# Four-layer kernel: ternary gate and up weights rounded into spent SBUF, and the first codes, turns and gate product of layer 1's feed-forward moved into the attention before it

## The chip, the cores and the metric

The kernel runs on one core of one Trainium2 chip. The time is device microseconds of one launch; the kernel's number is the median of three runs. TensorE is called PE in rows, VectorE DVE, ScalarE ACT, GpSimd POOL, and SyncE, which issues the DMAs, SP.

## What is computed

The input x has 2 x 256 rows of 512, in the kernel four tiles of 128 rows (0 and 1 are the first batch). Four layers follow, each an attention-like part and a feed-forward part on a layer norm of x, both added to x. The change touches layer 1: the end of its attention (a latent attention with 16 heads over 512 context rows) and its feed-forward part, which uses 4-bit and 8-bit activations and ternary weights. Cut to what matters:

```python
def int4_quant(x):
    beta = mean(abs(x), axis=-1)
    x_q = clip(round(x * SQRT7 / (beta + EPS)), -8, 7)
    return x_q * (beta * SQRT7) / SQRT7
def int8_quant(x):
    gamma = max(abs(x), axis=-1)
    x_q = clip(round(x * 127.0 / (gamma + EPS)), -128, 127)
    return x_q * gamma / 127.0
def bitlinear(x, w, scale):
    w_mean = mean(abs(w))
    w_q = clip(round(w / (w_mean + EPS)), -1.0, 1.0)
    return einsum('...i,oi->...o', x, w_q * w_mean * scale)
# layer 1, feed-forward, on h = layernorm(x):
#   gate, up = bitlinear(int4_quant(h), w_gate), bitlinear(int4_quant(h), w_up)   512 -> 1376
#   inner    = relu(gate)**2 * up
#   x        = x + bitlinear(int8_quant(inner), w_down)                           1376 -> 512
```

## The kernel before

Each part of a layer is one block: every engine has its own instruction stream, written out by hand in program order, synchronised by semaphores, and all engines meet at a barrier between two blocks. There is no planner; an engine executes its instructions in the order in which they are written.

**Ternary weights.** `TernaryWeights` holds 13 pieces: four of w_gate, four of w_up (128 x 1376 each) and five of w_down (three of 128 x 1536, then 128 x 512 and 96 x 512). Each is loaded twice into one of two raw buffers `tw_raw`: first for the sum of magnitudes, then, during layer 1's attention, for rounding. The second pass is `ternary_round_gpsimd` (lines 391 to 405): three operations of GpSimd for each piece, the last of which writes bf16 codes into one of two buffers `tw_rounded`, while `ternary_round_sync` (line 408) issues the store of each piece to DRAM (`ternary`) and the next load. In the feed-forward block SyncE loads all codes back (lines 1263 to 1269): `wgu` for gate and up in six DMAs, `wd` for down in two; then the first weights of layer 2's key/value and query products.

**The attention's end.** `layer1_attention` goes through 64 units u (tile u // 16, head u % 16). In unit u TensorE makes the scores of unit u + 3, turns the probabilities of u (line 978) and mixes four heads at a time (`mix`, line 994); VectorE takes the maximum of unit u + 3 (line 1072) and copies every fourth turned unit (line 1096); ScalarE does the exponential of u + 2 (line 1176) and the other copies (line 1185). A tile's result is copied by ScalarE (`copy_mixed`), turned by TensorE (`turn_mixed`, line 1008), divided and added to x by VectorE (lines 1082 and 1089). The norm statistics of tiles 0 to 2 are made in units 26, 42 and 58, their inverse roots by GpSimd behind all rounding, their normed rows `xn` by VectorE in units 59, 60 and 62 (`tile_rows_vector`, line 267).

**The feed-forward block.** `layer1_ffn`, for tiles t and the three column chunks c of 1376 (512, 512, 352):

- ScalarE sums the magnitudes of the normed rows (line 1290); VectorE makes the 4-bit codes of two tiles at a time (`quantise4`, lines 1333 to 1353: three small operations, two each of scale, round and clip of 128 x 512, three small ones for the scales), and behind the second pair come four counts of a bisection that belongs to layer 3 (line 2396); TensorE turns the codes (`turn4`, line 1424) and ScalarE copies them out.
- `gate_up(t)` (line 1453): for each chunk eight matmuls, gate and then up, into two banks each; it may write chunk i when ScalarE and VectorE have read chunk i - 2. ScalarE makes relu and square (lines 1311 and 1316), VectorE multiplies with up (`inner_chunk`, line 1365).
- VectorE: `magnitude(t)` (line 1370, the maximum over 1376, and four small ones), `scaled(t)` (line 1380), `rounded(t)` (line 1385), with the chunks of tile t + 1 in between. TensorE turns the 8-bit codes (`turn8`, line 1437), ScalarE copies them in two halves (lines 1300 to 1303), `down(t)` (line 1466) multiplies, and VectorE adds to x (`update`, line 1389).
- TensorE's order of calls is: gate_up 0, turn4 2, turn4 3, gate_up 1, turn8 0, gate_up 2, down 0, turn8 1, gate_up 3, down 1, turn8 2, a first product of layer 2, down 2, another, turn8 3, another, down 3. GpSimd meanwhile splits the loaded weights of layer 2 (`first_group_split`, lines 1524 to 1533).
- The updates of tiles 2 and 3 stand at the start of the next block (line 2295).

## Time and profile before

| what | us |
|---|---|
| median of 3 runs (lowest, highest) | 849.52 (848.99, 854.66) |
| profiled execution | 852.24 |
| its span | 850.5 |
| busy TensorE, VectorE, ScalarE, GpSimd in the span | 773.9, 688.9, 517.5, 431.8 |

The span runs from the first to the last instruction of the profiled execution; times inside it count from its start. Layer 1's attention ends at about 184 us of it, the feed-forward block at about 231.8.

### The profile page before, as it was taken

What the parts mean: (1) busy time and instruction counts of PE and PEld (TensorE: products, weight loads), DVE (VectorE), ACT (ScalarE), POOL (GpSimd) and SP (SyncE); (2) the same over time, 40 slices, a digit from 0 to 9 for tenths busy, and PEclk for the clock granted to TensorE, in tenths of its full rate; (3) what the DMA queues carried; (4) which work ended last, traced back from release to release, by engine and by line L of the source; (5) the groups of instructions that cost most, each with busy time, mean ns of one, the idle gap of its engine ahead of it and who ended that gap; (6) DMA issues with size and microseconds to landing.
All of it is one profiled execution on the core that took longest, in us unless ns stands there. A gap on an engine that the chain in (4) does not pass through costs nothing. (4 is left out here: it accounts for less than half of the span.)

```text
span 850.5 us, 16376 instructions
## 1 busy us (share of the span) xinstructions
PE 773.9 (91%) x5134; PEld 629.5 (74%) x5140; DVE 688.9 (81%) x1766; ACT 517.5 (61%) x1401; POOL 431.8 (51%) x388
## 2 busy tenths in 40 slices
PE   1986799948988999999999999999999999978888
PEld 0484676634677898888888888989888889866347
DVE  7877898979787887887887888788878878876986
ACT  6865789846457657657657656665675675641421
POOL 3136158824135754755746646745754764665110
PEclk9998899989999999999999999999999999999999
DMA  8245136635020320220220320310310210004001
GB/s 308 100 132 180 53 137 217 195 113 184 12 89 1 101 76 1 99 74 0 99 74 0 99 74 0 99 62 13 99 50 25 74 50 25 26 1 120 2 0 50
DMA packets 37773, 66.15 MB, mean 78 GB/s; under 512 B 5537, under 2 KB 17889, under 8 KB 37602
## 3 DMA queue, kind: packets, MB, share of 16 engines
q1 hardware_dynamic: 37730, 65.63, 23.2%
q8 instruction: 21, 0.34, 0.2%
q14 instruction: 22, 0.18, 0.1%
HBM read 60.28 MB, written 5.34 MB: 77 GB/s over the span
## 5 line engine op out<-in xcount | busy, mean ns | idle before, releaser
L2396 DVE TENSOR_SCALAR_CACHE_REDUCE xn<-ctxT,candidate 128x512 bf16<-128x512 f32 x240 | 168.9, 742 | 0.0
L2043 ACT ACTIVATE layer_attention_probs<-xnT,stats 128x512 f32<-128x512 f32 x128 | 93.9, 733 | 113.5 <-DVE stats L2178 113.5
L2190 DVE TENSOR_TENSOR layer_attention_probsT<-bank,layer_attention_probsT 128x512 fp32r<-128x512 f32 x128 | 88.2, 689 | 50.5 <-ACT layer_attention_probsT L2051 49.3
L1782 PE MATMUL bank<-layer_attention_keysT,layer_attention_queriesT 128*128 128x512 f32 x384 | 121.1, 423 | 4.9 <-DVE layer_attention_queriesT L2171 4.9
L1782 PEld LDWEIGHTS bank<-layer_attention_probsT,layer_attention_values 128*128 128x128 f32 x768 | 99.1, 190 | 13.7 <-DVE layer_attention_probsT L2190 4.2
L2051 ACT CAST layer_attention_probsT<-bank 128x512 fp32r<-128x512 f32 x128 | 74.9, 585 | 52.8 <-PE bank L1859 52.8
L1782 PE MATMUL bank<-layer_attention_probsT,layer_attention_values 128*128 128x256 f32 x768 | 102.6, 283 | 4.4 <-DVE layer_attention_probsT L2190 2.2
L1782 PE MATMUL bank<-layer_attention_l_wq,layer_attention_xnT 128*128 128x512 f32 x408 | 99.3, 392 | 0.1
L1782 PEld LDWEIGHTS bank<-layer_attention_l_wkv,layer_context_parts 128*128 128x128 f32 x720 | 88.4, 188 | 2.7
L1782 PE MATMUL bank<-layer_attention_l_wkv,layer_context_parts 128*128 128x256 f32 x720 | 90.4, 278 | 0.0
L1782 PE MATMUL bank<-layer_attention_wo,layer_attention_headsT 128*128 128x512 f32 x336 | 88.8, 406 | 0.0
L2178 DVE CUSTOM_DVE_ANT_0 xnT<-bank,layer_attention_mask 128x512 f32<-128x512 f32 x128 | 87.2, 681 | 0.6 <-PE bank L1782 0.5
L1782 PEld LDWEIGHTS bank<-layer_attention_l_wq,layer_attention_xnT 128*128 128x128 f32 x408 | 75.3, 188 | 15.9 <-issue 0.2
L1725 POOL TENSOR_TENSOR layer_attention_mixed<-layer_attention_mixed,xnT 128x512 f32<-128x512 f32 x30 | 49.1, 1637 | 69.9 <-DVE candidate L2446 41.7
L1859 PE MATMUL bank<-ident,layer_attention_probs 128*128 128x128 f32 x512 | 76.9, 272 | 3.0 <-ACT layer_attention_probs L2043 3.0
L1859 PEld LDWEIGHTS bank<-ident,layer_attention_probs 128*128 128x128 f32 x512 | 61.3, 140 | 14.4 <-issue 4.0
L1782 PEld LDWEIGHTS bank<-layer_attention_keysT,layer_attention_queriesT 128*128 128x128 f32 x384 | 62.6, 190 | 11.4 <-issue 5.7
L1782 PEld LDWEIGHTS bank<-layer_attention_wo,layer_attention_headsT 128*128 128x128 f32 x336 | 60.0, 189 | 11.5
L1710 POOL TENSOR_SCALAR layer_attention_ssq<-layer_attention_ssq 128x4 f32<-128x4 f32 x48 | 9.7, 203 | 87.5 <-ACT layer_attention_squares L2002 87.5
L2002 ACT ACTIVATE layer_attention_squares<-bank 128x128 f32<-128x128 f32 x192 | 52.0, 298 | 0.0
L1712 POOL TENSOR_TENSOR layer_attention_ssq<-layer_attention_ssq,minus_half 128x4 f32<-128x4 f32 x48 | 48.9, 1018 | 4.0
L1715 POOL TENSOR_TENSOR xn<-xn,layer_attention_ssq 128x512 f32<-128x512 f32 x47 | 48.9, 1040 | 3.7
(340 smaller groups left out, 1639.6 us busy)
## 6 DMA issues: line engine op xcount, KB each, us to landing
layer_attention_l_raw_qo<-in_wqT SPq DMA_DIRECT2D x8, 1024.0 KB, 5.5
layer_attention_l_raw_qo<-in_woT SPq DMA_DIRECT2D x8, 1024.0 KB, 6.0
xnT<-inverse_sums SPq DMA_DIRECT2D x15, 512.0 KB, 3.7
tw_raw<-in_w_gateT SPq DMA_DIRECT2D x8, 688.0 KB, 5.4
tw_raw<-in_w_upT SPq DMA_DIRECT2D x8, 688.0 KB, 4.3
tw_raw<-in_w_downT SPq DMA_DIRECT2D x6, 768.0 KB, 4.7
layer_attention_l_raw_kv<-in_wkvT SPq DMA_DIRECT2D x8, 512.0 KB, 4.7
ternary<-tw_rounded SPq DMA_DIRECT2D x8, 344.0 KB, 2.6
```

Source lines behind the costliest of these rows:

```text
L1710: own(g.tensor_scalar(ssq[:, c, :], ssq[:, c, :], 1.0 / HD, EPS, ALU.mult, ALU.add))
L1712: own(g.tensor_tensor(ssq[:, c, :], ssq[:, c, :], k.minus_half[:, 0:REP], ALU.pow))
L1715: g.tensor_tensor(r, r, ssq[:, c, :].unsqueeze(2).broadcast_to([P, REP, HD]), ALU.mult)\
L1725: g.tensor_tensor(now, now, factors, ALU.mult).then_inc(S_["mix_scaled"], 1)
L1782: last = pe.matmul(out, stationary[f][a], moving[f][b], start=f == 0 and x == 0, stop=f == count - 1 and x == 2)
L1859: last = pe.transpose(T[u % 2][:, c * P:(c + 1) * P], probs[:, u % 3, c * P:(c + 1) * P], k.ident[:, :])
L2002: return a.activation(squares[:, h, :], source, ACT.Square, accum_out=ssq[:, c, h:h + 1])
L2043: a.activation(probs[:, u % 3, :], masked[:, u % 2, :], ACT.Exp, bias=negmax[:, u:u + 1], scale=-1.0, accum_out=sums[:, u:u + 1]).then_inc ...
L2051: a.copy(probsT[:, 0, p % 2, :, u % 2 * P:(u % 2 + 1) * P], T[u % 2][:, :].rearrange("p (c q) -> p c q", c=CPB)).then_inc(S_["probsT_high" ...
L2178: v.tensor_tensor_reduce(masked[:, u % 2, :], S[u % 2][:, :], mask[:, u % TPB, :], -1.0, 3.4e38, ALU.add, ALU.min, negmax[:, u:u + 1]).the ...
L2190: v.tensor_tensor(probsT[:, 1, p % 2, :, columns], T[u % 2][:, :].rearrange("p (c q) -> p c q", c=CPB), probsT[:, 0, p % 2, :, columns], A ...
L2396: own(k.nc.vector.tensor_scalar((k.flags if flags is None else flags)[:, r % 2], row_tile(k.ctxT, r), k.candidate[:, r:r + 1].bitcast(F32) ...
```

## The change

- The gate and up codes no longer go through DRAM. GpSimd writes them straight into their place in SBUF (`GateUp.weights`), which lies over buffers that the attention has done with. Pieces are rounded in a new order (`ROUNDED`): down first, then up and gate. Piece 0 waits until all queries are made, piece 6 until the first batch's values are used. Only the down codes are stored and loaded back. GpSimd makes the inverse roots of tiles 0 and 1 between pieces.
- The 4-bit codes of tiles 0 and 1 are made in the attention block: one magnitude sum on ScalarE in unit 60, the other on VectorE in unit 61, the rest of the codes on VectorE in unit 62 and behind unit 63; their buffers lie over spent queries. TensorE turns them behind the last `mix`, ScalarE copies them behind its last `copy_mixed`, and TensorE does the first chunk of gate and up of tile 0 as the block's last work, with a wait for all 13 rounded pieces.
- In the feed-forward block the normed rows of tile 2 are made at the start, those of tile 3 behind the first `inner` chunk; the codes of tiles 2 and 3 come within VectorE's work on tile 1 (between its chunks 1 and 2), that is, behind tile 0's 8-bit codes. TensorE does down 0 and turns the late codes ahead of gate_up 2. The four counts move to the end of VectorE's stream. GpSimd's split waits until the late codes' scales are ready.

In the following rows a name such as `layer_attention_codes` is a tile, `x8` at a row's end a count of equal instructions. First TensorE, before, from the last mixing products of the attention into the feed-forward block:

```order
L994 MATMUL bank<-layer_attention_probsT,layer_attention_values 32x128 x24
L1008 MATMUL bank<-ident,layer_attention_mixedT 128x128 x4
L925 UNCONDITIONAL_BRANCH
L1417 UNCONDITIONAL_BRANCH
L1424 MATMUL bank<-ident,layer_ffn_x 128x128 x8
L1453 MATMUL bank<-layer_ffn_wgu,layer_ffn_x4T 128x512 x16
L1453 MATMUL bank<-layer_ffn_wgu,layer_ffn_x4T 128x352 x8
```

The same place of TensorE's stream now (`layer_attention_turned` holds the turned codes of tiles 0 and 1, `layer_attention_gate_up` the gate and up weights):

```order
L1119 MATMUL bank<-layer_attention_probsT,layer_attention_values 32x128 x24
L174 MATMUL bank<-ident,layer_attention_codes 128x128 x8
L1133 MATMUL bank<-ident,layer_attention_mixedT 128x128 x4
L190 MATMUL bank<-layer_attention_gate_up,layer_attention_turned 128x512 x8
L1047 UNCONDITIONAL_BRANCH
L1523 UNCONDITIONAL_BRANCH
L190 MATMUL bank<-layer_attention_gate_up,layer_attention_turned 128x512 x8
L190 MATMUL bank<-layer_attention_gate_up,layer_attention_turned 128x352 x8
```

The turns of the codes and the first eight products now stand ahead of the two branches, which are the border of the blocks.

VectorE, before, in tile 1 of the feed-forward block, from the scaling of tile 0 to the maximum of tile 1:

```order
L1380 TENSOR_SCALAR layer_ffn_inner<-layer_ffn_inner,layer_ffn_ginv 128x1376
L1365 SCALAR_TENSOR_TENSOR layer_ffn_inner<-bank,layer_ffn_up_scale,layer_ffn_gate 128x512
L1385 TENSOR_SCALAR layer_ffn_x<-layer_ffn_inner 128x1376
L1365 SCALAR_TENSOR_TENSOR layer_ffn_inner<-bank,layer_ffn_up_scale,layer_ffn_gate 128x512
L1365 SCALAR_TENSOR_TENSOR layer_ffn_inner<-bank,layer_ffn_up_scale,layer_ffn_gate 128x352
L1370 TENSOR_REDUCE layer_ffn_gamma<-layer_ffn_inner 128x1
```

The same place now, from the second chunk of tile 1 on:

```order
L1464 SCALAR_TENSOR_TENSOR layer_ffn_inner<-bank,codes_up_scale,layer_ffn_gate 128x512
L135 TENSOR_SCALAR codes_beta<-codes_beta 128x2
L137 TENSOR_SCALAR codes_betae<-codes_beta 128x2
L139 RECIPROCAL codes_binv<-codes_betae 128x2
L145 TENSOR_SCALAR layer_ffn_t<-xn,codes_binv 128x512 x2
L151 TENSOR_SCALAR layer_ffn_t<-layer_ffn_t 128x512 x2
L157 TENSOR_SCALAR layer_ffn_x<-layer_ffn_t 128x512 x2
L162 TENSOR_SCALAR codes_betae<-codes_beta 128x2
L164 TENSOR_SCALAR codes_up_scale<-codes_betae,tw_wscale 128x2
L165 TENSOR_SCALAR codes_gate_scale<-codes_betae,tw_wscale 128x2
L1464 SCALAR_TENSOR_TENSOR layer_ffn_inner<-bank,codes_up_scale,layer_ffn_gate 128x352
L1469 TENSOR_REDUCE layer_ffn_gamma<-layer_ffn_inner 128x1
```

The codes of tiles 2 and 3 have moved from the block's start to between the second and third chunk of tile 1.

The diff, cut to its core:

```diff
@@ TernaryWeights @@
+    ROUNDED = (8, 9, 10, 11, 12, 4, 5, 0, 1, 2, 3, 6, 7)
+    OVER_QUERIES, OVER_VALUES = 0, 6
...
+        k.gate_up = GateUp(k, -(-k.nc.sbuf_base // 32) * 32)
@@ ternary_round_gpsimd @@
-    for i, (w, f, rows, width) in enumerate(tw.PIECES):
...
-        g.tensor_scalar(tw.rounded[0:rows, n % 2, 0:width], raw, -ROUND, 1.0, ALU.add, ALU.mult)\
-         .then_inc(tw.rounded_ready, 1)
+        if w == DOWN:
+            if j >= 2:
+                g.wait_ge(tw.stored[n % 2], 16 * (j // 2))
+            target = tw.rounded[0:rows, n % 2, 0:width]
+        else:
+            if tw.ROUNDED[j] == tw.OVER_QUERIES:
+                g.wait_ge(queries_made, B * HEADS1 // 2)
+            if tw.ROUNDED[j] == tw.OVER_VALUES:
+                g.wait_ge(quads_done, TPB * HEADS1 // 4)
+            target = k.gate_up.weights[:, w, f, :]
+        g.tensor_scalar(target, raw, -ROUND, 1.0, ALU.add, ALU.mult).then_inc(tw.rounded_ready, 1)
@@ layer1_attention, gpsimd @@
-                ternary_round_gpsimd(k)
-                for t in range(TILES - 1):
-                    tile_norm_gpsimd(k, following, t)
+                ternary_round_gpsimd(k, 0, 6, S_["queries_psum"], S_["quads_done"])
+                tile_norm_gpsimd(k, following, 0)
+                ternary_round_gpsimd(k, 6, 10, S_["queries_psum"], S_["quads_done"])
+                tile_norm_gpsimd(k, following, 1)
+                ternary_round_gpsimd(k, 10, len(TernaryWeights.PIECES), S_["queries_psum"], S_["quads_done"])
+                tile_norm_gpsimd(k, following, 2)
@@ layer1_attention, tensor @@
                 mix(UNITS // 4 - 1, range(CPB))
+                for t in range(TPB):
+                    codes_turn_tensor(k, t, early_codes[t], code_bank(t))
                 turn_mixed(TILES - 1)
+                pe.wait_ge(k.codes.turned_ready, 1)
+                pe.wait_ge(k.ternary.rounded_ready, len(TernaryWeights.PIECES))
+                gate_up_tensor(k, 0, 0)
@@ layer1_attention, vector @@
-                    if u in (59, 60, 62):
-                        tile_rows_vector(k, following, (59, 60, 62).index(u))
+                    if u in (59, 60):
+                        tile_rows_vector(k, following, (59, 60).index(u))
+                    if u == 61:
...
+                        v.tensor_reduce(k.codes.beta[:, 1:2], k.xn[:, 1, :], AX.X, ALU.add, apply_absolute_value=True)\
+                         .then_inc(k.codes.beta_ready, 1)
+                    if u == 62:
+                        codes_inverse_vector(k, 0)
+                        codes_scaled_vector(k, 0, scaled)
...
+                codes_rounded_vector(k, 0, scaled)
+                codes_clipped_vector(k, 0, scaled, early_codes)
+                codes_scales_vector(k, 0)
                 divide_mixed(TILES - 1)
                 add_mixed(TILES - 1)
@@ layer1_attention, scalar @@
+                    if u == 60:
+                        codes_magnitude_scalar(k, following, 0, absolute)
...
                 copy_mixed(TILES - 1)
+                for t in range(TPB):
+                    codes_turned_scalar(k, t, code_bank(t))
@@ layer1_ffn, sync @@
-                for c, (c0, c1) in enumerate(CHUNKS):
-                    for w in (GATE, UP):
-                        sp.dma_start(wgu[:, w, :, c0:c1], tw.scratch[w].rearrange("(f p) c -> p f c", p=P)[:, :, c0:c1])\
-                          .then_inc(loaded[c], 16)
@@ layer1_ffn, gpsimd @@
+                g.wait_ge(q.scales_ready, 2)
                 first_group_split(k)
@@ layer1_ffn, scalar @@
                     if t == 0:
-                        x4T_copy(2)
-                        x4T_copy(3)
+                        for late in range(TPB, TILES):
+                            codes_magnitude_scalar(k, n, late, absolute[:, late - TPB, :])
                     if t >= 1:
                         x8T_copy(t - 1)
+                    if t == 1:
+                        codes_turned_scalar(k, 2, code_bank(2))
+                        codes_turned_scalar(k, 3, code_bank(3))
@@ layer1_ffn, vector @@
-                quantise4(0)
-                tile_rows_vector(k, n, TILES - 1)
-                quantise4(1)
+                tile_rows_vector(k, n, 2)
...
-                bisection_count(k, own, 0, first_flags(k))
-                for c in range(NC):
-                    inner_chunk(0, c)
-                    if c == 0:
-                        bisection_count(k, own, 1, first_flags(k))
+                inner_chunk(0, 0)
+                tile_rows_vector(k, n, TILES - 1)
+                inner_chunk(0, 1)
+                inner_chunk(0, 2)
...
+                    if t == 0:
+                        codes_inverse_vector(k, 1)
+                        codes_scaled_vector(k, 1, scaled_late)
+                        codes_rounded_vector(k, 1, scaled_late)
+                        codes_clipped_vector(k, 1, scaled_late, codes_late)
+                        codes_scales_vector(k, 1)
...
+                bisection_count(k, own, 0, first_flags(k))
                 for t in range(TPB):
                     tile_rows_vector(k, following, t)
+                bisection_count(k, own, 1, first_flags(k))
@@ layer1_ffn, tensor @@
                 gate_up(0)
-                turn4(2)
-                turn4(3)
                 gate_up(1)
                 turn8(0)
+                down(0)
+                codes_turn_tensor(k, 2, codes_late[0], code_bank(2))
+                codes_turn_tensor(k, 3, codes_late[1], code_bank(3))
                 gate_up(2)
-                down(0)
                 turn8(1)
                 gate_up(3)
                 down(1)
```

The functions `codes_...` are the old `quantise4`, `turn4` and `x4T_copy` taken apart; `gate_up_tensor` is the body of the old loop for one chunk.

## Rows read from the trace of the kernel before

**Rows 1.** Busy us by stretch: PE, PEld, DVE, ACT, POOL; PE clock, DMA share, GB/s

```profile
170.00:184.00 14.00, 9.35 (x131) 5.85 (x129) 9.81 (x25) 6.93 (x17) 4.19 (x7) 1.00 0.11 35
184.00:192.30 8.30, 1.91 (x11) 1.23 (x13) 6.57 (x22) 3.63 (x10) 0.57 (x1) 0.50 0.88 272
192.30:231.80 39.50, 36.38 (x222) 20.51 (x224) 32.41 (x61) 21.23 (x38) 13.34 (x10) 0.98 0.29 91
```

**Rows 2.** Waits in 184 to 200 us: total us, times, longest

```profile
PE bank L1424 <- DVE layer_ffn_x L1347: 6.3, 1, 6.3
```

**Rows 3.** Timeline of the attention's end: start, length in us, instruction, idle before

```profile
176.89 0.69 ACT L1176 ACTIVATE layer_attention_probs<-bank,layer_attention_negmax 128x512 f32<-128x512 f32 x1
181.52 0.63 PE L1008 MATMUL bank<-ident,layer_attention_mixedT 128*128 128x128 f32 x4 [0.80 <-ACT layer_attention_mixedT L1192]
```

**Rows 4.** Timeline of the feed-forward block's start, DVE and PE

```profile
184.25 0.69 DVE L257 BATCH_NORM_STATS2 stats<-x 128x6 f32<-128x512 f32 x1 [0.59 <-PEq L925]
190.53 0.17 DVE L1333 TENSOR_SCALAR layer_ffn_beta<-layer_ffn_beta 128x2 f32<-128x2 f32 x1 [0.79 <-ACT layer_ffn_t L1290]
194.13 0.74 DVE L2396 TENSOR_SCALAR_CACHE_REDUCE xnT<-ctxT,candidate 128x512 bf16<-128x512 f32 x1
191.42 4.78 PE L1453 MATMUL bank<-layer_ffn_wgu,layer_ffn_x4T 128*128 128x512 bf16 x15 [1.99 <-ACT layer_ffn_x4T L1285]
198.35 3.61 PE L1453 MATMUL bank<-layer_ffn_wgu,layer_ffn_x4T 128*128 128x512 bf16 x16 [0.19 <-DVE layer_ffn_inner L1365]
```

**Rows 5.** Groups by shape in 184 to 232 us: count, busy us, mean ns, idle before

```profile
L1311 ACT ACTIVATE layer_ffn_relu<-bank,layer_ffn_gate_scale 128x512 f32<-128x512 f32 x8 | 5.5, 690 | 3.3 <-PE bank L1453 3.2
L1290 ACT ACTIVATE layer_ffn_t<-xn 128x512 f32<-128x512 f32 x4 | 2.5, 621 | 6.5 <-DVE xn L267 3.6 <-PEq L925 2.9
L1365 DVE SCALAR_TENSOR_TENSOR layer_ffn_inner<-bank,layer_ffn_up_scale,layer_ffn_gate 128x512 f32<-128x512 f32 x8 | 6.0, 744 | 1.3 <-ACT layer_ffn_gate L1316 1.3
```

**Rows 6.** Timeline: the four `magnitude` starts, VectorE's largest gap, the block's end

```profile
198.96 1.59 DVE L1370 TENSOR_REDUCE layer_ffn_gamma<-layer_ffn_inner 128x1 f32<-128x1376 f32 x1
205.43 1.59 DVE L1370 TENSOR_REDUCE layer_ffn_gamma<-layer_ffn_inner 128x1 f32<-128x1376 f32 x1
212.03 1.59 DVE L1370 TENSOR_REDUCE layer_ffn_gamma<-layer_ffn_inner 128x1 f32<-128x1376 f32 x1
216.44 0.75 DVE L1365 SCALAR_TENSOR_TENSOR layer_ffn_inner<-bank,layer_ffn_up_scale,layer_ffn_gate 128x512 f32<-128x512 f32 x1 [1.34 <-ACT layer_ffn_gate L1316]
221.00 1.59 DVE L1370 TENSOR_REDUCE layer_ffn_gamma<-layer_ffn_inner 128x1 f32<-128x1376 f32 x1
220.90 0.78 PE L1437 MATMUL bank<-ident,layer_ffn_x 128*128 128x128 bf16 x11
228.86 2.55 PE L1466 MATMUL bank<-layer_ffn_wd,layer_ffn_x8T 128*128 128x512 bf16 x10
231.85 0.75 DVE L2295 SCALAR_TENSOR_TENSOR x<-bank,down_scale,x 128x512 f32<-128x512 f32 x1 [3.62 <-PEq L1259]
```

**Rows 7.** Timeline of GpSimd: its first rounding operation and the first behind all

```profile
112.97 1.48 POOL L400 TENSOR_SCALAR tw_raw<-tw_raw,tw_bound 128x1376 f32<-128x1376 f32 x1 [25.23 <-DVEq L388]
175.13 1.58 POOL L274 TENSOR_TENSOR rstd<-varep,minus_half 128x1 f32<-128x1 f32 x3
```

**Rows 8.** Line 1385 on VectorE (ns min/median/max), and GpSimd's split on the timeline

```profile
L1385 DVE TENSOR_SCALAR layer_ffn_x<-layer_ffn_inner x4: 867/992/1281, 202.6 to 224.1; 128x1376 bf16<-128x1376 f32 x4
203.06 3.01 POOL L1527 TENSOR_TENSOR layer_attention_l_wkv<-layer_attention_l_raw_kv,layer_attention_l_wkv 128x512 fp32r<-128x512 f32 x2
```

**Rows 9.** Busy us by stretch, as in rows 1, in the attention's first part

```profile
96.00:98.00 2.00, 0.42 (x3) 0.42 (x4) 1.94 (x4) 0.78 (x2) 0.00 (x0) 1.00 0.34 94
98.00:100.00 2.00, 2.00 (x17) 1.21 (x16) 1.97 (x4) 1.60 (x3) 0.00 (x0) 0.66 0.01 4
```

**Rows 10.** DMA issues: count, KB each, median us from issue to landing

```profile
layer_ffn_wd<-ternary SPq DMA_DIRECT2D x1, 1280.0 KB, 10.3
tw_raw<-in_w_upT SPq DMA_DIRECT2D x7, 688.0 KB, 4.3
```

More of the change, by code:

```diff
@@ new lines, in codes_scales_vector @@
+def codes_scales_vector(k, h):
+    v, own, q, half, wscale = k.nc.vector, k.vown, k.codes, half_of(h), k.ternary.wscale
+    own(v.tensor_scalar(q.betae[:, half], q.beta[:, half], SQRT7, 1.0 / SQRT7, ALU.mult, ALU.mult))
+    own.wait()
+    own(v.tensor_scalar(q.up_scale[:, half], q.betae[:, half], wscale[:, UP:UP + 1], None, ALU.mult))
+    own(v.tensor_scalar(q.gate_scale[:, half], q.betae[:, half], wscale[:, GATE:GATE + 1], None, ALU.mult))
+    own.wait()
+    v.engine_nop().then_inc(q.scales_ready, 1)
@@ new lines, in codes_turn_tensor, with codes_turned_scalar @@
+def codes_turn_tensor(k, t, codes, bank):
+    pe = k.nc.tensor
+    pe.wait_ge(k.codes.codes_ready, t + 1)
+    for f in range(KT):
+        last = pe.transpose(bank.bitcast(BF16)[:, f * P:(f + 1) * P], codes[:, f * P:(f + 1) * P], k.ident16[:, :])
+    last.then_inc(k.codes.turned_psum, 1)
+def codes_turned_scalar(k, t, bank):
+    a = k.nc.scalar
+    a.wait_ge(k.codes.turned_psum, t + 1)
+    a.copy(k.gate_up.turned[t], bank.bitcast(BF16).rearrange("p (f c) -> p f c", f=KT)).then_inc(k.codes.turned_ready, 1)
@@ L105, in at, with gate_up_tensor @@
+def gate_up_tensor(k, t, c):
+    pe, q = k.nc.tensor, k.codes
+    c0, c1 = INNER_CHUNKS[c]
+    i = len(INNER_CHUNKS) * t + c
+    for w, bank, ready in ((GATE, k.bank[0:2], q.gate_psum), (UP, k.bank[2:4], q.up_psum)):
+        for f in range(KT):
+            last = pe.matmul(bank[i % 2][:, 0:c1 - c0], k.gate_up.turned[t][:, f, :], k.gate_up.weights[:, w, f, c0:c1],
+                             start=f == 0, stop=f == KT - 1)
+        last.then_inc(ready, 1)
 def at(step, per, c):
@@ L286, with __init__, place @@
 GATE, UP, DOWN = range(3)
+INNER_CHUNKS = [(c, min(c + 512, INNER)) for c in range(0, INNER, 512)]
+class GateUp:
+    def __init__(self, k, base):
+        self.begin = base + 4 * KT * (2 * GW2 + 2 * 2 * HD2 + 2 * HD2 + GW2)
+        self.held = 2 * 2 * KT * INNER
+    def place(self, k):
+        view = lambda name, shape, offset: k.nc.alloc_sbuf_tensor_at(k.label + name, [P] + shape, BF16,
+                                                                     offset=self.begin + offset)
+        self.weights = view("gate_up", [2, KT, INNER], 0)
+        early = view("turned", [KT, TPB * P], self.held)
+        self.turned = [early[:, :, t * P:(t + 1) * P] for t in range(TPB)]
 class TernaryWeights:
@@ L2884, in build @@
 def build(nc, dram, out):
-    ternary = [nc.dram_tensor(f"ternary{w}", (INNER, D) if w == DOWN else (D, INNER), BF16, kind="Internal").ap()
-               for w in range(3)]
+    ternary = nc.dram_tensor("ternary", (INNER, D), BF16, kind="Internal").ap()
     inverse = nc.dram_tensor("inverse_sums", (P, 8), F32, kind="Internal").ap()
```

201 lines of the change are left out of this document (97 added, 104 removed).

## The prediction

> **What bounds the kernel now.** I read the views in the order in which they narrow down. The table by stage comes first [rows 1]: from 170 to 184 us (the end of layer 1's attention) and from 192.3 to 231.8 us (its feed-forward part, FFN below) TensorE is busy, but between them, 184.0 to 192.3, it works 1.91 of 8.30 us at a granted clock of 0.50, while the DMA engines are busy 0.88 of the time. The list of waits says for what: one wait of 6.3 us for `layer_ffn_x`, the 4-bit codes that VectorE makes [rows 2]. The first long product starts at 191.42, two more microseconds on, and its 15 matmuls take 4.78 us; 16 of the same kind take 3.61 us at full clock [rows 4]. So the boundary is a serial chain: sum of magnitudes on ScalarE, codes on VectorE, transposes, copy, first product, and all of it behind the barrier between two blocks. After it the FFN is bound by VectorE (32.41 of 39.50 us) and TensorE (36.38) by turns [rows 1]. The next stage starts when TensorE's last product of the FFN is done: VectorE waits 3.62 us for that barrier [rows 6]. From there on the program is unchanged, so what the boundary and the FFN give goes through to the end. Nothing else of the 850 us has to be looked at but the gaps on GpSimd before [rows 7].
>
> **The end of the attention: what is added.** ScalarE gets one magnitude sum (0.62 us by the mean of four [rows 5]) between exponential 62 and the copy of turn 60. It paces this stretch: the last exponential, at 176.89, shows no idle time of ScalarE ahead of it [rows 3], so 0.6 us goes onto the path to the last mixing product. VectorE gets a reduction, the three small operations and the six of 128x512 of the codes: the group from its first small operation at 190.53 to the next work at 194.13 takes 3.60 us [rows 4]. The reduction and the first part fit into its idle time before the last copy of turned probabilities, the rest while TensorE mixes and ScalarE copies; I count nothing for it. If it were not hidden at all, it would cost all 3.6. TensorE turns eight 128x128 of codes in the time in which it waited for the copy of the mixed rows, up to its transpose at 181.52 [rows 3]; then, behind that transpose and ScalarE's copies of the turned codes, eight matmuls of 128x512, half of 3.61, 1.8 us. VectorE's division and addition of the last tile run beside them; I put TensorE's end 0.5 us after theirs. Nothing is queued behind this product in the block, but the barrier waits for it. Sum: the barrier moves from 184.25 to about 185.35, +1.1. Bounds: +0.6 (product hidden) to +4.7 (codes not hidden).
>
> **GpSimd and SyncE.** GpSimd rounds the 13 pieces from 112.97 to 175.13, 62.2 us, loads included [rows 7]. The order of pieces changes, the arithmetic does not; eight stores of 344 KB to DRAM and the six loads back go. Two of its three inverse roots move in between the pieces, each wanted only near 175.7. SyncE issues a load behind fewer stores. I leave the end at 175, within 3 either way. The new wait, the first gate product for all 13 pieces, then ends 8 us before TensorE comes to it, at about 183: no cost. The waits for spent queries and spent values stand at pieces 8 and 12 of the row, at about 149 and 168, when the first half of the attention is over; none either. In the FFN SyncE issues the down weights first. Before they landed 10.3 us after the issue, behind the gate and up weights [rows 10]; even with that they are there at 196, and the first down product wants them at 197.
>
> **The start of the FFN.** VectorE at 185.35: statistics of tile 3 (0.69 and two short ones, as the 0.17 at 190.53), rows of tile 2 (taken as 0.55, under the 0.74 of an `inner` chunk), the first `inner` chunk (0.74) [rows 4, 5]. That ends at 187.8 and lets TensorE into the third chunk. Half of its matmuls (352/512 of half of 1.8 us, 0.6), relu and square (each under the 0.69 of a relu of 512 columns [rows 5]), the last chunk of `inner`: `magnitude(0)` starts at 190.25, where it stood at 198.96 [rows 4, 6]. The lead is 8.7 us. It is made of the codes and their turns that are gone from here (to 191.42), the half clock, the four counts behind 194.13, and it pays the 1.1.
>
> **What is given back.** The codes of tiles 2 and 3 now stand between two chunks of tile 1: +3.60 to 205.43 - 198.96 = 6.47 [rows 6], less what that stretch holds beyond its instructions, a wait for ScalarE and GpSimd's interference, which I put at 0.7: 9.3 us. Lead 5.9. Tile 2's product can only start when its codes are turned behind the first down product, at about 200.3; by my schedule `magnitude(2)` then comes at 206.45 against 212.03, lead 5.6. Between `magnitude(2)` and `magnitude(3)` there were 8.97 us, in part because TensorE did the first down product ahead of the second turn; that product now lies earlier, and I get 7.95: lead 6.6. The four counts (2.9 us with the gaps) now stand at VectorE's end, where it waited 3.62 us for TensorE [rows 6]: they are hidden with about 1 us to spare. TensorE's tail, from its turn at 220.90 to the end of the last down product (228.86 and 2.55), takes 10.5 us and is unchanged; it starts at 214.1, after the last gate and up products at 211.7 and 2.4 us of down product, 6.8 earlier. I take a gain of 6.5 at the FFN's end (6.3 by the ready times of the last codes, 6.8 by the tail).
>
> **Interference.** The operation that rounds 128x1376 to codes took 0.87 us at best and 1.28 at worst [rows 8], the slow ones beside GpSimd's split of the next weights (two operations in 3.01 us). Before three such pairs (scale or round) lay beside the split, now four. By these rows that is 0.1 to 0.4 us more, inside my rounding. The Trainium skill ("SBUF — State Buffer", the term "shared port pair") says that VectorE and GpSimd lock that pair for a whole instruction and that the loser fully blocks. By that rule the extra operation could stand behind one whole split operation, 1.5 us, and the time would be 844.5 rather than 843.0. The rows, with 0.41 us as the largest excess, speak for the smaller figure.
>
> **Sum.** +1.1 at the barrier, -9.8 from the barrier to `magnitude(0)`, +2.8 for the late codes, about -0.6 for the order of TensorE: -6.5 us. The profiled execution took 852.24 us (span 850.5); it becomes 845.7. The median shown, 849.52, lies 2.72 lower: 843.0 us. That is 0.77% less. A measurement of this kernel can tell about 1% (8.5 us) from no change.
>
> **Rivals.**
> (a) The clock falls. Between 96 and 98 us TensorE was busy 0.42 of 2 us, and the next two microseconds had a clock of 0.66 [rows 9]; between 184 and 192.3 it was 0.50 [rows 1]. The new boundary still has a barrier, a wait for the first `inner` and waits of about 1 us in tiles 0 and 1. At half clock a product of eight takes 3.4 instead of 1.8 us; two of them on the path are 3.2 us: 846.2. Against it: no new gap is as long as 2 us. The Trainium skill ("TensorE: Matmul & The Clock Gate", What's actually happening) says that throttled is the default and activity lifts it; that speaks for neither here without the trace.
> (b) The lead carries through. If TensorE's new order and the early start of the down product take the 3.6 us of late codes into waits that were there anyway, 8.7 or more remains: 840.8. For it: VectorE idled 3.62 at the end. Against it: the largest gap of VectorE inside the FFN is 1.34 us, at 216.44 [rows 6].
> (c) Slower: the rounding ends late. Place: TensorE's wait for all 13 pieces at about 183, with the next block's barrier behind it. The loads of one piece are hidden behind the rounding of another only by two buffers. If each of the eight gate and up pieces waited for a whole landing of 4.3 us [rows 10], GpSimd would end 34 us late, at 209, and the time be 843 + 26 = 869. It costs nothing up to 183 and turns the gain over from an end at 189.5. Against it: the whole 62.2 us held 13 pieces with only short gaps [rows 7], and DMA traffic gets less. Gaps of 2 us behind the two small pieces are to be expected.
>
> **How the numbers follow.** Forecast 60%, with its own range 841 to 845.5: each of four stretches is good to about 1 us. (a), together with codes not wholly hidden in the attention's end, 20%, up to 848. (b) 16%, from 839 to 841. (c) 4%. The range 839 to 848 leaves out (c), the far end of (a), where both bounds meet (+4.7 at the barrier and a fallen clock), and the far end of (b). Faster by over 1% means below 841.0: (b) and the edge of the forecast, 0.2. Slower by over 1%: (c), 0.04. Within 1%: 0.76.
>
> **What would show it.** The next profile should have the wait of 6.3 us gone, the granted clock near 1.00 from 184 to 200, the first gate product ending at about 184.7 with GpSimd done at 175, `magnitude` starts near 190.3, 199.6, 206.5 and 214.4, the late codes of 3.6 us between two chunks, and the first operation of layer 2 on VectorE at about 225.4 with a short wait. The prediction is wrong if GpSimd's last piece comes after 183, if the barrier comes after 187, or if the stage behind the FFN gets longer by what the FFN saved.

## The result: faster by half a per cent, two waits larger than forecast

The changed kernel takes 848.77 us (median of 13 runs, 844.14 to 851.61) beside 853.23 us for the kernel before in the same session (13 runs, 848.99 to 855.45): ratio 0.9949, 95% interval 0.9928 to 0.9971. Timed again later it was 847.13 beside 852.7, ratio 0.9938 (0.9917 to 0.9959). So the gain is 4.5 to 5.6 us; the forecast was 6.5 us, ratio 0.9923, and an absolute time of 843.0 with a range that ended at 848. Of the absolute miss of 5.8 us, 3.7 are the yardstick: the kernel before has 849.52 in the three runs shown ahead of the prediction, 853.23 in the 13 runs beside the changed kernel, and medians of 851 to 853 in later sessions. The other 2 us are gain that didn't come.

The profiled execution took 848.75 us, span 846.6. VectorE on the timeline, against [rows 4, 6]: start, length, instruction, idle time ahead of it.

```profile
187.43 0.69 DVE L347 BATCH_NORM_STATS2 stats<-x 128x6 f32<-128x512 f32 x1 [0.66 <-PEq L1047]
192.42 1.59 DVE L1469 TENSOR_REDUCE layer_ffn_gamma<-layer_ffn_inner 128x1 f32<-128x1376 f32 x1
201.78 1.59 DVE L1469 TENSOR_REDUCE layer_ffn_gamma<-layer_ffn_inner 128x1 f32<-128x1376 f32 x1
209.19 1.59 DVE L1469 TENSOR_REDUCE layer_ffn_gamma<-layer_ffn_inner 128x1 f32<-128x1376 f32 x1
217.23 1.59 DVE L1469 TENSOR_REDUCE layer_ffn_gamma<-layer_ffn_inner 128x1 f32<-128x1376 f32 x1
227.76 0.75 DVE L2386 SCALAR_TENSOR_TENSOR x<-bank,down_scale,x 128x512 f32<-128x512 f32 x1 [1.16 <-PEq L1397]
```

Executions differ by up to 5 us in where they stand at 170 us, together with dips of the granted clock ahead of it, and by almost 5 us behind the FFN. So I compare distances and not positions, from a mark that both kernels have: VectorE's reading of the fourth count in the attention's last part, which starts at 170.90 in the kernel before and at 170.12 in the changed one. All distances are from start to start, in us:

| | count to barrier | to magnitude(0) | (0) to (1) | (1) to (2) | (2) to (3) | to layer 2 | sum |
|---|---|---|---|---|---|---|---|
| before | 13.35 | 14.71 | 6.47 | 6.60 | 8.97 | 10.85 | 60.95 |
| forecast | 14.45 | 4.9 | 9.3 | 6.9 | 7.95 | 11.0 | 54.5 |
| changed | 17.31 | 4.99 | 9.36 | 7.41 | 8.04 | 10.53 | 57.64 |
| changed, again | 17.69 | 5.00 | 9.35 | 7.41 | 8.03 | 10.53 | 58.01 |

In these steps the changed kernel gains 3.3 and 2.9 us, less than the medians' 4.5 and 5.6; the rest lies outside them, and no run here says where it comes from.

Four of six steps are right within 0.5 us. Two are not: 2.9 us too much ahead of the barrier, 0.5 between magnitude(1) and (2). The first is seen on the timeline of the changed kernel, all engines, rows of the bisection's update, of GpSimd's rounding and of what waits:

```profile
170.12 0.08 DVE L2487 DVE_READ_ACCUMULATOR xn<-ctxT,candidate 128x1 f32 x1
170.43 1.41 POOL L509 TENSOR_SCALAR tw_raw<-tw_raw,tw_winv 128x1376 f32<-128x1376 f32 x1
170.66 1.20 DVE L2534 TENSOR_TENSOR found<-found,set_bit 128x8 int32<-128x8 int32 x1
171.93 1.34 POOL L521 TENSOR_SCALAR layer_attention_gate_up<-tw_raw 128x1376 bf16<-128x1376 f32 x1
171.97 1.31 DVE L2537 TENSOR_TENSOR candidate<-found,bits 128x8 int32<-128x8 int32 x1
173.92 0.69 ACT L1316 ACTIVATE layer_attention_probs<-bank,layer_attention_negmax 128x512 f32<-128x512 f32 x1 [4.36 <-DVE layer_attention_negmax L1202]
174.75 0.80 PE L1095 MATMUL bank<-l_keysT,layer_attention_queriesT 128*128 128x512 f32 x1 [3.60 <-ACT layer_attention_probs L1316]
```

Two operations on eight columns take 1.20 and 1.31 us. Each ends where the GpSimd operation beside it ends (170.43 + 1.41 = 171.84; 171.93 + 1.34 = 173.27). Behind them VectorE's maximum is late, ScalarE idles 4.36 us, TensorE 3.60. In the kernel before the same two lines on the timeline are

```profile
171.41 0.17 DVE L2443 TENSOR_TENSOR found<-found,set_bit 128x8 int32<-128x8 int32 x1
171.69 0.17 DVE L2446 TENSOR_TENSOR candidate<-found,bits 128x8 int32<-128x8 int32 x1
```

and GpSimd was idle there, in a gap of 2.33 us in which it waited for the small last down piece, between 170.58 and 172.91. The change puts the gate and up pieces last and so a wide rounding under the update. The busy table by stretch of the changed kernel (columns as in [rows 1]) shows the granted clock fall behind TensorE's idle piece, from 1.00 in [rows 1] to 0.75, while 184 to 192.4 runs at 1.00 and not at 0.50:

```profile
170.60:184.00 13.40, 9.54 (x114) 6.26 (x113) 12.05 (x26) 6.87 (x18) 3.13 (x3) 0.75 0.00 0
184.00:192.40 8.40, 7.43 (x43) 3.58 (x42) 6.20 (x15) 5.65 (x11) 0.78 (x1) 1.00 0.42 143
192.40:227.80 35.40, 30.73 (x199) 17.73 (x197) 33.14 (x64) 18.27 (x34) 13.24 (x10) 1.00 0.16 52
```

The second excess lies beside GpSimd's split; VectorE and GpSimd on the timeline of the changed kernel, against [rows 8]:

```profile
202.29 2.50 POOL L1618 TENSOR_TENSOR layer_attention_l_wkv<-layer_attention_l_raw_kv,layer_attention_l_wkv 128x512 fp32r<-128x512 f32 x2
203.91 1.62 DVE L1479 TENSOR_SCALAR layer_ffn_inner<-layer_ffn_inner,layer_ffn_ginv 128x1376 f32<-128x1376 f32 x1
204.73 2.55 POOL L1621 CAST layer_attention_l_wq<-layer_attention_l_raw_qo 128x2048 fp32r<-128x2048 f32 x1
206.11 1.90 DVE L1484 TENSOR_SCALAR layer_ffn_x<-layer_ffn_inner 128x1376 bf16<-128x1376 f32 x1
219.36 0.94 DVE L1479 TENSOR_SCALAR layer_ffn_inner<-layer_ffn_inner,layer_ffn_ginv 128x1376 f32<-128x1376 f32 x1
220.33 0.88 DVE L1484 TENSOR_SCALAR layer_ffn_x<-layer_ffn_inner 128x1376 bf16<-128x1376 f32 x1
```

The same two operations take 1.62 and 1.90 us for tile 1, 0.94 and 0.88 for tile 3, where GpSimd is idle. Over tiles 1 and 2 the excess is 2.2 us (1.62 + 1.90 + 1.02 + 1.28 against twice 0.94 + 0.87). The kernel before already has 0.8 of it: 1.11 us for rounded(0), 1.08 for scaled(1), 1.28 for rounded(1). So the change adds 1.4.

### The profile page after: what moved, and what is told of

Same layout as the page of the kernel before. It is cut to its first block and busy times, and to the rows that moved or that the text cites. A ratio compares the mean times of both kernels' runs of the same rounds, so it can differ in the third digit from the quotient of the medians.

```text
span 846.6 us, 16363 instructions
## 1 busy us (share of the span) xinstructions
PE 776.7 (92%) x5140; PEld 633.9 (75%) x5140; DVE 692.8 (82%) x1767; ACT 517.6 (61%) x1399; POOL 431.9 (51%) x388
## 5 line engine op out<-in xcount | busy, mean ns | idle before, releaser
L2142 ACT CAST layer_attention_probsT<-bank 128x512 fp32r<-128x512 f32 x128 | 75.0, 586 | 54.7 <-PE bank L1950 54.5
L1873 PE MATMUL bank<-layer_attention_l_wkv,layer_context_parts 128*128 128x256 f32 x720 | 93.5, 282 | 0.0
L1873 PEld LDWEIGHTS bank<-layer_attention_l_wkv,layer_context_parts 128*128 128x128 f32 x720 | 91.1, 188 | 2.5
L1316 ACT ACTIVATE layer_attention_probs<-bank,layer_attention_negmax 128x512 f32<-128x512 f32 x64 | 44.8, 705 | 11.8 <-DVE layer_attention_negmax L1202 11.5
```

Of the source, the lines that this page charges most:

```text
L1316: a.activation(probs[:, u % 4, :], S[u % 3][:, :], ACT.Exp, bias=negmax[:, tile(u), head(u):head(u) + 1], accum_out=sums[:, tile(u), head( ...
L1873: last = pe.matmul(out, stationary[f][a], moving[f][b], start=f == 0 and x == 0, stop=f == count - 1 and x == 2)
L2142: a.copy(probsT[:, 0, p % 2, :, u % 2 * P:(u % 2 + 1) * P], T[u % 2][:, :].rearrange("p (c q) -> p c q", c=CPB)).then_inc(S_["probsT_high" ...
```

## The experiments

Ratios are to the kernel before, run in the same session. Those of the single edits and of the changed kernel have intervals that overlap, so what one edit is worth is read from the steps of its trace, and the time only says whether it fits.

**Repeat of the changed kernel.** No edit.

> The changed kernel as it is, on the same chip as the three others, to compare them with. Theory A: the operation found<-found,set_bit takes over 1 us in this profile too and TensorE's idle piece ahead of the down products' end is there again (3 us or more); ratio to the kernel before 0.993 to 0.997. Theory B (the long operations were this one execution's): about 0.17 us each, and a time near the forecast of 843.

Measured: 847.13 us, ratio 0.9938 (0.9917 to 0.9959). The two operations take 1.20 and 1.31 us again, TensorE idles 3.59 us behind them. The wait belongs to the kernel, not to one execution: in all five profiles that leave this place as it is, `found` takes 1.19 or 1.20 us and `candidate` 1.31.

**The update moved to the FFN.**

```diff
@@ attention, behind the fourth count
-                        if counts == 4:
-                            bisection_update(k, own)
@@ FFN, VectorE
                 inner_chunk(0, 1)
+                bisection_update(k, own)
                 inner_chunk(0, 2)
```

> The changed kernel with the bisection's update (found, candidate and their compares, ten small VectorE operations) taken out of the attention's end and put between inner_chunk(0,1) and inner_chunk(0,2) of the FFN, where GpSimd is idle and VectorE had an idle piece of 0.88 us. Theory A (the small operations found<-found,set_bit and candidate<-found,bits wait until the GpSimd rounding beside them is through): they take about 0.17 us each in their new place instead of 1.20 and 1.31; TensorE's idle piece of 3.60 us before 174.75 and the clock of 0.65 to 0.80 behind it are gone; from the stretch's last count to the barrier 14.0 to 14.5 us instead of 17.2, the rest as in the changed kernel; a time of about 845.5 us beside 848.8, ratio to the kernel before about 0.991. Theory B (the 2.2 us came with this execution, or stem from what follows the update): the idle piece and the barrier stay, ratio 0.995.

Measured: 844.65 us, ratio 0.9912 (0.9886 to 0.9938). On its timeline:

```profile
183.20 0.17 DVE L2533 TENSOR_TENSOR found<-found,set_bit 128x8 int32<-128x8 int32 x1
183.49 0.17 DVE L2536 TENSOR_TENSOR candidate<-found,bits 128x8 int32<-128x8 int32 x1
```

Count to barrier 13.02 us, 1 us less than expected, all later steps within 0.01 of the changed kernel's; sum 53.35. The granted clock is 1.00 from 160 to 188. Theory A holds. But this edit takes the update's own time from the stretch too, so it can't yet say what the wait alone costs.

**The last piece rounded in quarters.** The update stays where it is.

```diff
+        size = width // 4 if j == len(tw.ROUNDED) - 1 else width
+        parts = [raw[:, i:i + size] for i in range(0, width, size)]
+        for part in parts:
-        k.pown(g.tensor_scalar(raw, raw, tw.bound[...], ALU.min, ALU.max))
+            k.pown(g.tensor_scalar(part, part, tw.bound[...], ALU.min, ALU.max))
...
```

(and the same for the other two operations of a piece.)

> The changed kernel, where the last of the 13 pieces is rounded in quarters of 344 columns: 12 instructions of about 0.6 us in place of three of 1.48, 1.41 and 1.34, so about 3 us more of GpSimd. The update stands where it stood. Theory A (each small operation waits to the end of the one GpSimd instruction beside it): found and candidate take at most 0.65 us each, their starts and ends stand at the ends of GpSimd's instructions, TensorE's idle piece is 1 to 2 us shorter than 3.60. Theory B (they wait until GpSimd pauses, or all of its work on the piece slows them): they take as long as before or longer, 1.2 us and more.

Measured: 844.15 us, ratio 0.9911 (0.988 to 0.9941). Its timeline, VectorE, GpSimd and TensorE:

```profile
165.11 2.47 POOL L510 TENSOR_SCALAR tw_raw<-tw_raw,tw_bound 128x344 f32<-128x344 f32 x4
166.49 0.47 DVE L2537 SCALAR_TENSOR_TENSOR enough<-counts,flip 128x8 f32<-128x8 f32 x1
166.99 0.17 DVE L2539 TENSOR_TENSOR set_bit<-enough,bits 128x8 int32<-128x8 f32 x1
167.19 0.41 DVE L2541 TENSOR_TENSOR found<-found,set_bit 128x8 int32<-128x8 int32 x1
167.68 2.13 POOL L513 TENSOR_SCALAR tw_raw<-tw_raw,tw_winv 128x344 f32<-128x344 f32 x4
167.72 0.17 DVE L2544 TENSOR_TENSOR candidate<-found,bits 128x8 int32<-128x8 int32 x1
169.35 0.49 PE L1102 MATMUL bank<-l_keysT,layer_attention_queriesT 128*128 128x512 f32 x1 [1.92 <-ACT layer_attention_probs L1323]
```

The four quarters end at about 165.73, 166.35, 166.96 and 167.58 (2.47 / 4 each); `enough` ends at 166.96 and `found` at 167.60. These two wait for the GpSimd operation that runs, and for no more. Not every small operation waits: `set_bit` (166.99, a quarter begins at about 166.96) and here `candidate` (167.72, a quarter begins at 167.68) stand just behind the start of a GpSimd operation and take 0.17 us. The start alone doesn't settle it, since `candidate` waited 1.31 us in the changed kernel at the same distance (171.97 and 171.93); this stays open. Count to barrier is 14.44 us, which still holds 0.5 us of wait (0.47 and 0.41 in place of 0.17 each), so about 13.9 without any. The version with the update moved says the same: 13.02, and the update's 0.85 us (182.81 to 183.66 in its timeline) on top. The kernel before has 13.35: the added work costs the barrier 0.5 to 0.6 us, the rest of the changed kernel's 17.3 to 17.7 is the wait and its wake. GpSimd's operations on the last piece take about 2 us longer in sum, and the count to barrier is still 2.9 us shorter than in the changed kernel.

**The same wait in the kernel before.**

```diff
-    COUNT_AT = range(40, 60, 5)
+    COUNT_AT = range(36, 56, 5)
```

> The kernel before, with its four counts and the update behind them four units of the attention earlier (COUNT_AT 36, 41, 46, 51 in place of 40, 45, 50, 55), where GpSimd rounds a down piece without a break. Theory A (the small operations with two operands in SBUF wait for the GpSimd instruction that runs): found<-found,set_bit and candidate<-found,bits, 0.17 us each in the kernel before, take 0.5 to 1.6 us each here, in a kernel without anything of the change, and TensorE has an idle piece of 1 to 3 us behind them; the time 0 to 3 us more. Theory B (the change's gate and up pieces or its stores into the spent buffers make them long): 0.17 us each, and the time of the kernel before.

Measured: 854.31 us, ratio 1.0017 (0.9998 to 1.0035). Its timeline:

```profile
162.78 1.62 POOL L400 TENSOR_SCALAR tw_raw<-tw_raw,tw_bound 128x1536 f32<-128x1536 f32 x1 [0.38 <-DMA tw_raw<-in_w_downT]
163.43 0.99 DVE L2439 SCALAR_TENSOR_TENSOR enough<-counts,flip 128x8 f32<-128x8 f32 x1
164.50 1.54 POOL L402 TENSOR_SCALAR tw_raw<-tw_raw,tw_winv 128x1536 f32<-128x1536 f32 x1
164.65 1.40 DVE L2443 TENSOR_TENSOR found<-found,set_bit 128x8 int32<-128x8 int32 x1
166.17 1.44 DVE L2446 TENSOR_TENSOR candidate<-found,bits 128x8 int32<-128x8 int32 x1
169.08 0.50 PE L970 MATMUL bank<-l_keysT,layer_attention_queriesT 128*128 128x512 f32 x1 [3.43 <-ACT layer_attention_probs L1176]
```

The same stall, 3.43 us of TensorE, in a kernel without any of the change: theory B falls. The cost in time, 1.5 us of medians, is not told from nothing: the interval includes 1.

**GpSimd's split in four gated pieces.** Added lines without a call say in words what is split there.

```diff
                 g.wait_ge(q.scales_ready, 2)
-                first_group_split(k)
+                K and V high parts, first low part
+                g.wait_ge(x8_ready, 2)
+                second low part of K and V, Q high part
+                g.wait_ge(x8_ready, 3)
+                three low parts of Q
+                tile_norm_gpsimd(k, following, 0)
+                g.wait_ge(x8_ready, 4)
+                last low part of Q
```

> The changed kernel with GpSimd's split of K, V and Q cut into four pieces, each behind one of the semaphores of tiles 1 to 3, so that it no longer runs beside the whole-tile operations scaled and rounded of tiles 1 and 2. Theory A (these operations wait for GpSimd's instructions): scaled(1) 1.62 and rounded(1) 1.90 us go back to about 0.94 and 0.87, those of tile 2 from 1.02 and 1.28 to the same, magnitude(1) to magnitude(2) 6.0 to 6.8 us instead of 7.41; the time 1.0 to 2.2 us less than the changed kernel's, ratio to the kernel before 0.992 to 0.994. Theory B (TensorE ends each tile's turn, VectorE has slack there): the operations shorten, the starts of magnitude(2) and (3) stay within 0.3 us, ratio 0.995.

Measured: 846.96 us, ratio 0.992 (0.9897 to 0.9943). All four `scaled` take 0.94 and all four `rounded` 0.86 to 0.88; the whole 2.2 us of excess is gone. The steps: (1) to (2) 7.00 in place of 7.41, where I expected 6.0 to 6.8; (2) to (3) 7.53 in place of 8.04; but to layer 2 10.95 in place of 10.53. That is a gain of 0.5 us in the trace where 1.0 to 2.2 was expected, and the median is 0.2 us under the changed kernel's in the same session. TensorE tells why. Its turn of tile 2's 8-bit codes, in the changed kernel and in this version:

```profile
216.71 0.78 PE L1534 MATMUL bank<-ident,layer_ffn_x 128*128 128x128 bf16 x11
```

```profile
216.51 0.78 PE L1555 MATMUL bank<-ident,layer_ffn_x 128*128 128x128 bf16 x11
```

From there to layer 2 both need 11.05 us (to 227.76 and 227.56, the first addition of layer 2), and the turn itself comes 14.93 and 14.43 us behind magnitude(1). The tail hangs on TensorE, so of VectorE's lead of 0.9 us at magnitude(3) only 0.5 is left at layer 2. Theory A is right on the operations, theory B on half of what they are worth.

The count to barrier, where this version has no edit, is 16.54 us, although `found` and `candidate` wait as long as ever. The granted clock tells it apart: 0.64 and 0.93 from 176 to 184, where the changed kernel has 0.70, 0.50 and 0.95 from 172 to 184.

**Both edits.**

> Both edits at once: the update in the FFN, and the split in four gated pieces. If both waits are what the theory says and lie in different stretches, the gains add: 4 to 5 us less than the changed kernel, ratio to the kernel before about 0.990. If the second gain is only the first one seen from another side (TensorE late in both), the ratio is that of the update alone.

> The version with both edits once more, beside the one before: ratio to the kernel before 0.988 to 0.992, from the stretch's last count to the barrier 13.0 us, magnitude(1) to (2) 7.0 us.

Measured: 844.28 us, ratio 0.9897 (0.9875 to 0.9919), and 843.36 us, ratio 0.9892 (0.9863 to 0.9921). Steps 13.01, 5.00, 9.36, 7.00, 7.53, 10.95: the gains add, sum 52.85, 8.1 us under the kernel before. These are the lowest ratios of all that ran, lower than the changed kernel's 0.9949 and 0.9938. The few parts per thousand between it and the update's edit alone lie inside the intervals; the 0.5 us stand in the traces.

**The split without its gate.**

```diff
-                g.wait_ge(q.scales_ready, 2)
                 first_group_split(k)
```

> The changed kernel without GpSimd's wait for the late codes' scales ahead of the split, which so starts at about 195 instead of 201 us. Theory A (VectorE's wide operations wait for GpSimd's): the stretch beside which the split runs moves: scaled(0), rounded(0) and the late codes' three pairs of operations take 1.0 to 2.5 us each in place of 0.76 to 0.94, scaled(1) and rounded(1) go back towards 0.94 and 0.87; magnitude(0) to (1) 10 to 12 us in place of 9.3, magnitude(1) to (2) 6.8 to 7.2 in place of 7.4; the sum 0 to 2 us worse. Theory B (the long operations of tiles 1 and 2 are their own, for example by contention with TensorE's reads of the same buffers): scaled(1) stays at 1.62 and rounded(1) at 1.90 wherever the split stands.

Measured: 854.97 us, ratio 1.0028 (1.0008 to 1.0048): the whole gain is lost. Its timeline:

```profile
198.79 1.19 DVE L137 TENSOR_SCALAR codes_betae<-codes_beta 128x2 f32<-128x2 f32 x1
200.22 3.26 DVE L145 TENSOR_SCALAR layer_ffn_t<-xn,codes_binv 128x512 f32<-128x512 f32 x2
201.87 5.53 POOL L1623 TENSOR_TENSOR layer_attention_l_wq<-layer_attention_l_raw_qo,layer_attention_l_wq 128x512 fp32r<-128x512 f32 x4
203.51 2.77 DVE L151 TENSOR_SCALAR layer_ffn_t<-layer_ffn_t 128x512 f32<-128x512 f32 x2
206.31 1.70 DVE L157 TENSOR_SCALAR layer_ffn_x<-layer_ffn_t 128x512 bf16<-128x512 f32 x2
207.73 1.03 PE L174 MATMUL bank<-ident,layer_ffn_x 128*128 128x128 bf16 x8 [5.72 <-DVE layer_ffn_x L157]
```

The late codes' three pairs take 7.73 us; in the changed kernel 0.88 + 0.76 + 0.76 = 2.40. TensorE idles 5.72. Magnitude(0) to (1) is 16.63 us where I expected 10 to 12: I had counted the operations, one wait for each, and not that short operations alternate with GpSimd's, so that five of the six wait anew (1.4 to 1.9 us each; the last, behind the end of the split, takes 0.41). The long operations move with the split; they are not tile 1's own.

**The first gate product back behind the barrier.**

```diff
-                pe.wait_ge(k.codes.turned_ready, 1)
                 pe.wait_ge(k.ternary.rounded_ready, len(TernaryWeights.PIECES))
-                gate_up_tensor(k, 0, 0)
...
-                    for c in range(1 if t == 0 else 0, NC):
+                    for c in range(NC):
```

> The changed kernel with the first gate product (8 products of 512 columns, 1.9 us) behind the barrier again instead of in the attention's end. My reckoning: in the attention's end it lies beside VectorE's additions into x and costs the barrier nothing or at most 0.7 us; behind the barrier it stands on TensorE's way to tile 0's first chunk, so the barrier comes 0 to 0.7 us earlier and magnitude(0) 1.0 to 1.9 us later behind it: 0.5 to 1.9 us slower in sum. Rival (TensorE waits for the barrier anyway, and the FFN's start hangs on ScalarE's gates): no difference.

Measured: 850.15 us, ratio 0.9971 (0.9949 to 0.9994). Count to barrier 17.64, as in the changed kernel (17.31 and 17.69), and VectorE waits for the barrier 0.58 us without the product and 0.66 with it: it costs the barrier 0.1 us at most. Barrier to magnitude(0) 7.73 in place of 5.00: it is worth 2.7 us, more than its own 1.9 and than the 0.5 to 1.9 expected. In this version TensorE stands idle at the barrier (2.10 us), and the granted clock is 0.61 behind it. Busy times of this version by stretch, columns as in [rows 1]:

```profile
184.00:188.00 4.00, 3.45 (x9) 1.29 (x10) 1.62 (x5) 1.32 (x2) 0.78 (x1) 0.61 0.58 151
```

**The late codes ahead of tile 0's 8-bit codes.** On top of both edits.

```diff
                 inner_chunk(0, 2)
+                the six operations of the codes of tiles 2 and 3
                 for t in range(TILES):
...
                 gate_up(0)
+                codes_turn_tensor(k, 2, codes_late[0], code_bank(2))
+                codes_turn_tensor(k, 3, codes_late[1], code_bank(3))
                 gate_up(1)
```

> The version with both edits (update in the FFN, split in four gated pieces), where VectorE makes the codes of tiles 2 and 3 right behind inner_chunk(0,2), ahead of tile 0's 8-bit codes, and TensorE turns them between its products of tile 0 and tile 1: the order of the kernel before, as far as the late codes go. My reckoning (the late codes belong behind tile 0's 8-bit codes, as in the changed kernel): magnitude(0) comes 3.2 us later, magnitude(0) to (1) falls by less, 9.4 to 7 to 8 us, since TensorE waits for the turned codes ahead of its products of tile 1; 0.5 to 1.5 us slower than the version without this edit, ratio to the kernel before about 0.991. Rival (VectorE is the bound there and its work is the same in either order): no difference, ratio 0.990.

Measured: 851.42 us, ratio 0.9986 (0.9967 to 1.0006). Steps 13.02, 9.33, 7.07, 8.82, 7.54, 10.93, sum 56.71: 3.9 us more than the version without this edit. Nearly all of magnitude(0)'s delay of 4.3 us is kept: (0) to (1) falls by 2.3, (1) to (2) rises by 1.8. TensorE idles for the codes:

```profile
190.72 1.04 PE L174 MATMUL bank<-ident,layer_ffn_x 128*128 128x128 bf16 x8 [4.79 <-DVE layer_ffn_x L157]
```

So the direction was right and the size not. Of the delay of magnitude(0), 0.77 us are a wait of VectorE for ScalarE's sums of magnitudes, which I hadn't counted. This order in the change, tile 0's 8-bit codes first, is worth about as much in these steps as the whole change gains in them. The medians differ by 8 us, the traces by 3.9 in these steps, and the profiled executions of the two versions, taken side by side (851.08 and 848.21), by 2.9; the rest of the 8 is open.

## Why the prediction came out as it did

The sign, the class (within 1%) and the mechanism at the boundary of the blocks were right. The cost of the attention's end was not, and the time of 848.77 lies outside the range of 839 to 848. The yardstick's shift of 3.7 us alone is larger than the 0.8 us by which it does; the gain, 4.5 us in place of 6.5, is the miss that the steps explain. By its steps:

- **"The barrier moves from 184.25 to about 185.35, +1.1": this failed in the changed kernel, +3.96 and +4.34.** The added work costs 0.5 to 0.6 us, the lower of the two bounds ("product hidden"), and the version with the product behind the barrier agrees. What was missing is a wait of the update for GpSimd's rounding: 2.17 us directly (1.20 + 1.31 - 2 x 0.17), and 1.2 to 1.6 us (17.31 or 17.69, less 13.9 and 2.17) in its wake, where TensorE's clock had fallen. In the version with the gated split, whose clock was down for about half as long, the wake is 0.5 us (16.54). I took GpSimd's part as free once "the order of pieces changes, the arithmetic does not". I asked when the rounding ends and never what it runs beside.
- **"-9.8 from the barrier to magnitude(0)": right,** -9.72. The late wait of 6.3 us is gone, the clock there is 1.00.
- **"+2.8 for the late codes", (0) to (1) 9.3 us: right,** 9.36.
- **"0.1 to 0.4 us more, inside my rounding": wrong.** VectorE's operations take 1.4 us more than before (2.2 us of excess in place of 0.8). That costs 0.5 on the way to magnitude(2) against the forecast, and all 2.2 are worth 0.5 at the FFN's end, as the gated version shows. I took the largest excess in [rows 8] as a bound, though it only showed how far two operations happened to overlap there. The Trainium skill ("SBUF — State Buffer", the term "shared port pair"), against which I sided, states that the loser blocks for the whole instruction. The operations that waited agree, down to small ones that end within 0.02 us of GpSimd's, and the 1.4 us are near the 1.5 that the prediction worked out by that rule. Its section "Who interferes with whom" also names operations with two inputs in SBUF, which is the case of `enough`, `found` and `candidate`. The trace of before held the sign: line 1089, `x` plus the mixed rows, four times in 0.68 to 1.86 us (columns: ns min/median/max, first and last start), the longest at 166.59, beside a rounding that ended at 167.91 (166.44 + 1.47), 0.54 us ahead of its own end:

```profile
L1089 DVE TENSOR_TENSOR x<-x,layer_attention_mixed x4: 681/1094/1861, 125.2 to 183.0; 128x512 f32<-128x512 f32 x4
```
- **The tail:** 10.53 us where 11.0 were forecast, which hides 0.5 of the miss ahead of it; the four counts are hidden as said, VectorE waits 1.16 us behind them.
- **GpSimd done at 175, the new wait free:** done at 173.27 in the changed kernel. Right, and rival (c) is out.
- **The first gate product ends at about 184.7:** it ends at 186.98, 0.2 us behind VectorE's addition (186.07 + 0.69); the difference in position is the stall's.
- **Rival (a), a fallen clock,** came true in part, at another place: ahead of the barrier, at 172 to 180 us, behind a stall that it did not name. Rival (b) did not come true. The version without the two waits gives -8.1 us in the trace, near (b)'s -8.7, but not by (b)'s way: its late codes still take (0) to (1) to 9.36 us, and what it gains over the forecast comes mostly from the attention's end (13.01 in place of 14.45), which the update has left. That the sizes meet is chance.

Against the forecast's 54.5 us the changed kernel takes 57.64: +2.9 at the barrier, +0.5 between magnitude(1) and (2), -0.5 in the tail, +0.2 in small pieces. The 8.1 us of the best version and the ratio of 0.989 (9 us) agree as far as the intervals allow.

What stays open: the granted clock's dips outside this stretch, which come in some executions and not in others (40 to 56, 96 to 104, 236 to 276 and 756 to 792 us). Executions of the same kernel differ by up to 8 us; how much of that the dips cause, and what causes them, no run here shows.

## What to carry to other kernels

When a change moves work on GpSimd, list what VectorE does beside it in the new place, not only when GpSimd is done: a VectorE operation of 0.17 us can take 1.3. Small operations that sit on a chain (a bisection's update, a scale) belong where GpSimd is idle; if they can't move, cutting GpSimd's instructions beside them into shorter ones caps the wait at one of them. A spread in the durations of one line and shape, here 0.68 to 1.86 us, is where to look first. And follow a shortened operation to the engine that ends the stage: of 2.2 us taken off VectorE here, 0.5 reached the end.

## What the runs showed of the hardware that I had not expected

- VectorE operations on eight columns waited to the end of a running GpSimd operation on 1376 or 1536 columns: 1.20, 1.31, 1.40, 1.44 us in place of 0.17, and 0.41 beside quarters of 0.62. Some that began within 0.05 us of the GpSimd operation's start did not wait. It met `TENSOR_TENSOR` and `SCALAR_TENSOR_TENSOR` with both inputs in SBUF, and `TENSOR_SCALAR` (1.19 us on two columns, in the version without the gate).
- It goes both ways: GpSimd's cast of 128x2048 took 2.55 us beside `scaled(1)` and 1.88 in the version without the gate.
- The counts (`TENSOR_SCALAR_CACHE_REDUCE`, one SBUF input, 0.73 and 0.74 us) stood beside GpSimd's rounding and did not lengthen.
- With an idle piece of TensorE of 3.60 us that ended at 174.75, the granted clock was 0.70 from 172 to 176 and 0.50 from 176 to 180; with one of 1.92 us in the quartered version it stayed at 1.00.
